# Down products one unit later, and the third low up chunk on GpSimd, in a perceiver layer with a routed expert stage

## The chip, the cores and the metric

The kernel runs on one core of one Trainium2 chip. The metric is the device time in microseconds of one execution; of several executions the median is taken. Less is better.

## What is computed

One layer over 512 tokens of width 512 (`x`), in three parts that each add to `x`:

```
x = x + cross_attention(layernorm(x), ctx 8192 x 512, bias 512 x 8192)
x = x + causal_self_attention(layernorm(x))
x = x + moe(layernorm(x))          # the part that the change touches

moe:  scores = softmax(x @ gate_w.T)            # 8 experts, the best 2 of each token
      for each expert e:  g, u = x @ gate_up[e].T       # 2 x 704 wide
                          out += w[:, e] * ((silu(g) * u) @ down[e].T)
      out += sigmoid(x @ shared_gate) * shared(x)       # a shared expert of width 1408
```

The products are float32 in accuracy. Each float32 operand is split into a high part (a rounded copy of it in the type `fp32r`) and a low part (the operand less its high part, in `fp32r` too), and a product is three matrix multiplications: high by high, high by low, low by high.

## The kernel before, in words

**Stages.** The cross attention takes the first 60% of the time, the self attention follows, and then the expert stage. The shared expert is cut in 11 slices of 128 hidden columns each; eight of them (numbers 0 to 7) come before the routed experts and three after. Between them lie the routed **units**. A unit is 128 gathered token rows of one expert: `unit(u)` exists once in the program of each engine (lines 1329 for TensorE, 1905 for VectorE, 800 for ScalarE), and for GpSimd it is one turn of a loop with `down_last_low` and `send_home`. There are 8 units for the 8 experts, and up to 7 more for experts with over 128 rows. In the profiled inputs there are 3 more, so 11 units.

**One unit.** The up and gate weights of an expert come in three chunks c = 0, 1, 2 (256, 256 and 192 hidden columns, gate and up side by side: 2048, 2048 and 1536 numbers in each partition), and so do the down weights (1024 numbers in each partition). For each unit:

- SyncE issues the loads `raw_u[c]` (1, 1 and 0.75 MB) and `raw_d[c]` (0.5 MB each). There is one buffer of each, so a load waits until the low part of the weights before it has been made (`up_lo_ready`, `dn_lo_ready`, `dn_last_ready`). All loads stand in one order in SyncE's queue (`load_unit`).
- ScalarE copies the raw weights to their high parts (`up_high`, `down_high`), applies silu (`silu_e`), copies the turned hidden values to their high part (`hidden_high`), copies the gathered rows (`gathered_high`), and copies the finished result out of PSUM (`keep`, into the one buffer `y_out`).
- VectorE makes the low parts: of the up weights (`up_low`, or in two halves `up_low_half`), of the down chunks 0 and 1 (`down_low`), of the hidden values (`hidden_low`) and of the gathered rows (`gathered_low`), and it multiplies gate by up (`product_e`). The low parts of weights read two operands from SBUF. The others read one from SBUF and one from PSUM.
- GpSimd makes the low part of down chunk 2 (`down_last_low`, line 528), and sends the finished rows home with an indirect DMA (`send_home`, line 551): it waits until the rows of the unit before have landed, casts the row numbers (`home_s`), waits for `keep`, makes a one-element addition (`blank`) and issues the DMA.
- TensorE multiplies (`up`, `down`), turns the hidden values (`turn_hidden`) and the rows of the next unit (`turn_gathered`).

**Order.** The order on each engine is written out by hand, and every engine works strictly in order. TensorE in unit u: `up(u,0)`, `down(u-1,2)`, `turn_gathered(u+1)`, `up(u,1)`, `turn_hidden(u,0)`, `up(u,2)`, `turn_hidden(u,1)`, `down(u,0)`, `turn_hidden(u,2)`, `down(u,1)`. So the down products of a unit stand in the same unit, but for the third. `down_last_low(u)` holds a wait on `up_lo_ready` that lets it start only after the first up chunk of the next unit has its low part.

**Buffers of result.** `keep(u)` waits until all three down products of unit u are done and until the rows of unit u-1 have landed at home (`y_stored`), since there is one `y_out`. TensorE's first down product of the next unit waits for `keep` (`y_ready`), since there is one PSUM bank for the result.

Of the kernel before, what the change touches and what calls it, by code (L numbers as in the profile page):

```python
# [17 lines left out]
ST = S // P  # L18
# [32 lines left out]
def perceiver_layer(nc, x_in, stream1, ctx_in, wq_in, wk_in, wq_t_in, wk_t_in, bq_in, bk_in, wv_in, wqkv_in, gate_in, shared_in, up_in,  # L51
# [3 lines left out]
    with ExitStack() as scope:  # L55
# [178 lines left out]

        def turned_hidden(c):
            return ps[:, 3 + c, 0:2 * P]
# [48 lines left out]
        dn_last_ready = sem("dn_last_ready")  # L285
# [20 lines left out]
        def _(sp):  # L306
# [95 lines left out]
            def load_unit(u, expert_, expert_before, second=False, rows=True):  # L402
# [4 lines left out]
                if not second:  # L407
                    load_down(u - 1, expert_before, 2)
# [6 lines left out]
                load_down(u, expert_, 0)  # L415
                load_down(u, expert_, 1)
# [25 lines left out]
            load_down(extra + (E - 1), sp.value_load(last_expert[0:1, 0:1], min_val=0, max_val=E - 1), 2)  # L442
# [13 lines left out]
        def _(pool):  # L456
# [103 lines left out]

            down_last_low(0)
            pool.wait_ge(home_full, 16)
            pool.wait_ge(more_ready, 1)
            final = pool.value_load(more[0:1, 0:1], min_val=0, max_val=MORE) + (E - 1)
            send_home(0, first=True)
            down_last_low(1)
# [10 lines left out]
        def _(act):  # L577
# [203 lines left out]
            def silu_e(u, c):  # L781
                act.wait_ge(up_psum, u * CH + (c + 1))
                act.activation(gated_e[:, c, 0:WIDE[c]], ps[:, c % 2, 0:WIDE[c]], ACT.Silu).then_inc(silu_e_done, 1)
# [16 lines left out]
            def unit(u, first=False, second=False, last=False):  # L800
                silu_e(u, 0)
                down_high(u, 1)
                if not first:
                    keep(u - 1, first=second)
                if not last:
                    up_high(u + 1, 0)
                else:
# [4 lines left out]
                if not first:  # L812
                    act.wait_ge(y_psum_e, u * CH)
                down_high(u, 2)
                silu_e(u, 2)
                hidden_high(u, 1)
                if not last:
                    gathered_high(u + 1)
                    up_high(u + 1, 1)
                    hidden_high(u, 2)  # L820
                    up_high(u + 1, 2)
                    act.wait_ge(y_psum_e, u * CH + 1)
                    down_high(u + 1, 0)
                else:
                    hidden_high(u, 2)
# [28 lines left out]
            for n in range(LEAD):  # L854
# [9 lines left out]
                if n == LEAD - 2:  # L864
                    act.wait_ge(down_lo_ready, RAW)
                    up_high(0, 2)
            act.wait_ge(rows_out, 16 * 2 * ST)
            down_high(0, 0)
            gathered_high(0, bank=gate_bank(LEAD - 2))
            unit(0, first=True)  # L870
            unit(1, second=True)
            final = act.value_load(more[0:1, 0:1], min_val=0, max_val=MORE) + (E - 1)
            with act.Fori(2, final) as e:
                unit(e)
            unit(final, last=True)
            shared_sides_high(SH - 1)
# [11 lines left out]
        def _(pe):  # L888
# [398 lines left out]
            def up(u, c):  # L1287
                pe.wait_ge(xg_lo_ready, u + 1)
                pe.wait_ge(up_lo_ready, u * CH + (c + 1))
                out_ = ps[:, c % 2, 0:2 * WIDE[c]]  # L1290
# [38 lines left out]
            def unit(u, first=False, last=False, ahead=False):  # L1329
                if not first:  # L1330
                    pe.wait_ge(prod_e_done, u * CH)
                up(u, 0)
                if not first:
                    down(u - 1, 2)
                if first:
                    pe.wait_ge(added, 1)
                if not last:
                    turn_gathered(u + 1, ahead=ahead)
                if first:
                    pe.wait_ge(added, ST)  # L1340
                up(u, 1)
                turn_hidden(u, 0)
                up(u, 2)
                turn_hidden(u, 1)
                if not first:
                    pe.wait_ge(y_ready, u)
                down(u, 0)
                turn_hidden(u, 2)
                down(u, 1)
# [27 lines left out]
            unit(0, first=True, ahead=True)  # L1377
            for u in range(1, AHEAD_ROWS - 1):
                unit(u, ahead=True)
# [7 lines left out]
            down(final, 2)  # L1387
# [8 lines left out]
        def _(dve):  # L1396
# [452 lines left out]
            def up_low(u, c):  # L1849
                dve.wait_ge(up_hi_ready, u * CH + (c + 1))  # L1850
                dve.tensor_tensor(wu_lo[c][:, :, :], raw_u[c][:, :, :], wu_hi[c][:, :, :].bitcast(F32),
                                  ALU.subtract).then_inc(up_lo_ready, 1)
# [21 lines left out]
            def product_e(u, c):  # L1874
                dve.wait_ge(silu_e_done, u * CH + (c + 1))
                w = WIDE[c]
                h, g_, u_ = hid_e[:, c, 0:w], gated_e[:, c, 0:w], ps[:, c % 2, w:2 * w]
# [27 lines left out]
            def unit(u, first=False, last=False):  # L1905
                if first:
                    dve.wait_ge(down_done, LEAD + CREDIT)
                    for st in (2, 0, 1, 3):
                        add_shared(st)
                product_e(u, 0)  # L1910
                down_low(u, 1)
                if not last:
                    up_low_half(u + 1, 0, False)
                product_e(u, 1)
                hidden_low(u, 0)
                if not last:
                    up_low_half(u + 1, 0, True)
                product_e(u, 2)
                hidden_low(u, 1)
                if not last:  # L1920
                    gathered_low(u + 1)
                    up_low_half(u + 1, 1, False)
                    hidden_low(u, 2)
                    up_low_half(u + 1, 1, True)
                    up_low(u + 1, 2)
                    down_low(u + 1, 0)
                else:
                    hidden_low(u, 2)
# [22 lines left out]
            down_low(0, 0)  # L1951
# [96 lines left out]
```

## Time and profile before

| | |
|---|---|
| median of 3 runs | 686.71 us (685.3 to 690.03) |
| the profiled execution | 686.13 us, its span 684.4 us |
| TensorE busy | 678.1 us, 99% of the span |
| VectorE busy | 553.8 us, 81% |
| ScalarE busy | 340.3 us, 50% |
| GpSimd busy | 211.4 us, 31% |
| DMA | 134.33 MB moved, mean 196 GB/s |
| granted TensorE clock | 1.00 (2.4 GHz) over the whole span |

The routed units lie from 515.8 us to 658.9 us of the span. How to read it: busy time is the time in which an engine's instructions ran, whether they did work or were held up by something that the profile doesn't name; an "idle before" is time in which it waited, with the engine that ended the wait. L with a number is a line of the kernel. DVE is VectorE, ACT is ScalarE, POOL is GpSimd, PE is TensorE, SP is SyncE.

### The profile page before, as it was taken

Reading aid. Unit: us, or ns where it says so; the run is one execution under the profiler, and the core shown is the slowest. Engines: PE = TensorE matmul, PEld = TensorE weight load, DVE = VectorE, ACT = ScalarE, POOL = GpSimd, SP = SyncE. Lnnn points to the kernel's source line nnn. Section 1 sums busy time; section 2 is a strip of 40 time slices with the busy share of each in tenths; the row PEclk is TensorE's granted clock in tenths of the full one; section 3 lists DMA queues with packets and bytes.
Section 4 is the critical chain, followed back from the end, with each engine's and each line's share of the span. In section 5 each row is a group of like instructions: output and inputs, shape, how many; then the busy total and the mean of one; then the engine's idle time right before and its main releaser. Section 6 shows DMA issues by size and latency. Waiting matters only on the chain.

```text
span 684.4 us, 9739 instructions
## 1 busy us (share of the span) xinstructions
PE 678.1 (99%) x3156; PEld 562.4 (82%) x3156; DVE 553.8 (81%) x722; ACT 340.3 (50%) x460; POOL 211.4 (31%) x167
## 2 busy tenths in 40 slices
PE   8999999999999999999999999999999999999997
PEld 7788888888888788888888888888888888888886
DVE  6588898777979998899998662669658998998937
ACT  5522222222245565566665342652356888888830
POOL 4754445445440000000000000225762433434360
PEclk9999999999999999999999999999999999999999
DMA  8467767767742236422320330713267999999723
GB/s 288 190 202 230 227 219 234 252 221 229 256 148 93 93 118 250 186 92 92 101 83 0 155 139 0 307 47 112 106 203 271 338 363 369 382 377 394 269 91 124
DMA packets 41742, 134.33 MB, mean 196 GB/s; under 512 B 6576, under 2 KB 13104, under 8 KB 38384
## 3 DMA queue, kind: packets, MB, share of 16 engines
q1 hardware_dynamic: 39184, 127.39, 52.8%
q0 software_dynamic: 1520, 5.05, 1.9%
q10 hardware_dynamic: 1008, 1.51, 0.7%
q8 instruction: 17, 0.28, 0.2%
q14 instruction: 13, 0.11, 0.1%
HBM read 123.78 MB, written 10.15 MB: 196 GB/s over the span
## 4 chain that ended last, share of the span: by engine, by line
PE 94%; DVE 2%; DMA 2%; ACT 1%; issue 1%; DVEq 0%; ACTq 0%; SPq 0%
PE ps L1075 26%; PE ps L1017 9%; PE ps L1018 8%; PE ps L1021 8%; PE ps L1313 5%; PE ps L912 4%; PE ps L914 4%; PE ps L913 4%; PE ps L1270 4%; PE ps L1294 3%; PE ps L1292 3%; PE ps L1293 3%; PE ps L982 2%; PE ps L929 2%; DMA raw_u<-up_in 1%; PE ps L1202 1%
## 5 line engine op out<-in xcount | busy, mean ns | idle before, releaser
L492 POOL TENSOR_TENSOR c_lo<-ring,c_hi 128x512 fp32r<-128x512 f32 x64 | 87.0, 1362 | 86.0 <-ACT c_hi L639 86.0
L639 ACT ACTIVATE c_hi<-ring 128x512 fp32r<-128x512 f32 x64 | 40.5, 633 | 128.5 <-PE ps L1021 86.0
L509 POOL TENSOR_TENSOR w_lo<-raw,w_hi 128x1024 fp32r<-128x1024 f32 x11 | 27.5, 2497 | 248.2 <-ACT w_hi L762 236.0
L1017 PE MATMUL ps<-qk_hi,c_hi 128*128 128x512 f32 x256 | 99.9, 390 | 0.0
L1018 PE MATMUL ps<-qk_lo,c_hi 128*128 128x512 f32 x256 | 99.6, 389 | 0.0
L1509 DVE TENSOR_TENSOR runmax<-runmax,att 128x512 f32<-128x512 f32 x64 | 83.9, 1311 | 3.7
L1503 DVE SCALAR_TENSOR_TENSOR att<-ring,beta,ps 128x512 f32 (+1 forms) x64 | 47.8, 746 | 26.6 <-PE ps L1021 25.6
L1021 PE MATMUL ps<-qk_hi,c_lo 128*128 128x512 f32 x256 | 68.6, 389 | 0.0
L1075 PE MATMUL ps<-p_hi,d_hi 128*128 128x512 f32 x256 | 63.8, 391 | 0.0
L1075 PE MATMUL ps<-p_hi,d_lo 128*128 128x512 f32 x256 | 63.3, 389 | 0.0
L1075 PE MATMUL ps<-p_lo,d_hi 128*128 128x512 f32 x256 | 63.2, 389 | 0.0
L775 ACT ACTIVATE wu_hi<-raw_u 128x2048 fp32r<-128x2048 f32 (+1 forms) x33 | 58.6, 1777 | 6.7 <-DMA raw_u<-up_in 5.9
L1859 DVE TENSOR_TENSOR wu_lo<-raw_u,wu_hi 128x1024 fp32r<-128x1024 f32 x40 | 51.5, 1287 | 10.0 <-ACT wu_hi L775 9.6
L665 ACT ACTIVATE d_hi<-ring 128x1024 fp32r<-128x1024 f32 x32 | 33.9, 1060 | 50.1 <-PE ps L1075 49.3
L1017 PEld LDWEIGHTS ps<-qk_hi,c_hi 128*128 128x128 f32 x256 | 48.1, 188 | 10.7 <-DVE qk_lo L1477 0.7
L1021 PEld LDWEIGHTS ps<-qk_hi,c_lo 128*128 128x128 f32 x256 | 48.1, 188 | 10.0
L1075 PEld LDWEIGHTS ps<-p_hi,d_lo 128*128 128x128 f32 x256 | 48.0, 188 | 10.0
L1075 PEld LDWEIGHTS ps<-p_hi,d_hi 128*128 128x128 f32 x256 | 47.6, 188 | 10.6 <-DVE ps L1609 0.8
L1075 PEld LDWEIGHTS ps<-p_lo,d_hi 128*128 128x128 f32 x256 | 48.1, 188 | 10.0
L1018 PEld LDWEIGHTS ps<-qk_lo,c_hi 128*128 128x128 f32 x256 | 48.1, 188 | 9.8
L1292 PE MATMUL ps<-wu_hi,xg_hi 128*128 128x512 f32 (+1 forms) x132 | 51.0, 386 | 0.0
L1294 PE MATMUL ps<-wu_hi,xg_lo 128*128 128x512 f32 (+1 forms) x132 | 49.3, 373 | 0.0
(320 smaller groups left out, 1466.9 us busy)
## 6 DMA issues: line engine op xcount, KB each, us to landing
ring<-stream SPq DMA_DIRECT2D x64, 512.0 KB, 4.3
raw_u<-up_in SPq DMA_DIRECT2D x22, 1024.0 KB, 7.0
raw_d<-down_in SPq DMA_DIRECT2D x33, 512.0 KB, 7.7
ring<-ctx_in SPq DMA_DIRECT2D x32, 512.0 KB, 3.3
raw<-shared_in SPq DMA_DIRECT2D x11, 768.0 KB, 5.8
raw_u<-up_last_in SPq DMA_DIRECT2D x11, 768.0 KB, 7.8
slots<-blank SPq DMA_DIRECT2D x15, 264.0 KB, 5.1
late<-wqkv_in SPq DMA_DIRECT2D x1, 3072.0 KB, 10.6
```

Source lines behind the costliest of these rows:

```text
L492: pool.tensor_tensor(c_lo[:, s % 2, :], ring1[:, s, 0, :], c_hi[:, s % 2, :].bitcast(F32), ALU.subtract).then_inc(lo1_ready, 1)
L639: act.activation(c_hi[:, s % 2, :], ring1[:, s, 0, :], ACT.Copy).then_inc(hi1_ready, 1)
L775: act.activation(wu_hi[c][:, :, :], raw_u[c][:, :, :], ACT.Copy).then_inc(up_hi_ready, 1)
L1017: pe.matmul(ps[:, s, :], hi, qk_hi[:, k, :], start=(k == 0), stop=False)
L1018: pe.matmul(ps[:, s, :], hi, qk_lo[:, k, :], start=False, stop=False)
L1021: return pe.matmul(ps[:, s, :], c_lo[:, s % 2, k * P:(k + 1) * P], qk_hi[:, k, :], start=False, stop=(k == KC - 1))
L1075: mm = pe.matmul(ps[:, 4 + d, :], a[s % 2][:, t, d * P:(d + 1) * P], b[s % 2][:, t, :], start=(opening and t == 0), stop=False, skip_group ...
L1292: pe.matmul(out_, xg_hi[:, k, :], wu_hi[c][:, k, :], start=(k == 0), stop=False)
L1294: mm = pe.matmul(out_, xg_lo[:, k, :], wu_hi[c][:, k, :], start=False, stop=(k == KC - 1))
L1503: dve.scalar_tensor_tensor(out=att[:, g * U + s, :], in0=ring1[:, s, 1, :], scalar=beta[:, 0:1], in1=ps[:, s, :], op0=ALU.mult, op1=ALU.ad ...
L1509: dve.tensor_tensor(runmax[:, :], runmax[:, :], att[:, g * U + s, :], ALU.max).then_inc(max_done, 1)
L1859: ins = dve.tensor_tensor(wu_lo[c][:, k, :], raw_u[c][:, k, :], wu_hi[c][:, k, :].bitcast(F32), ALU.subtract)
```

## The change

TensorE's order in unit u becomes `up(u,0)`, `turn_hidden(u-1,2)`, `down(u-1,0)`, `up(u,1)`, `turn_hidden(u,0)`, `turn_gathered(u+1)`, `up(u,2)`, `down(u-1,1)`, `turn_hidden(u,1)`, `down(u-1,2)`: all three down products of a unit stand in the next unit. The third up chunk gets a PSUM bank of its own (7). The orders of ScalarE, VectorE and SyncE follow. The low part of the third up chunk is made by GpSimd (`up_last_low`) ahead of `down_last_low`, which loses its wait on the up chunk, and `send_home` comes after both. In short (lines of waits' counts left out where they only follow the new order):

```diff
+        up_bank = (0, 1, 7)
...
# SyncE
             def load_up(u, expert_, c, first=False):
                 if not first:
-                    sp.wait_ge(up_lo_ready, u * CH + (c + 1 - CH))
+                    if c < 2:
+                        sp.wait_ge(up_lo_ready, u * 2 + (c + 1 - 2))
+                    else:
+                        sp.wait_ge(up_last_ready, u)
...
                 load_up(u, expert_, 0)
                 if not second:
-                    load_down(u - 1, expert_before, 2)
+                    load_down(u - 1, expert_before, 0)
                 load_up(u, expert_, 1)
...
                 load_up(u, expert_, 2)
-                load_down(u, expert_, 0)
-                load_down(u, expert_, 1)
+                if not second:
+                    load_down(u - 1, expert_before, 1)
+                    load_down(u - 1, expert_before, 2)
...
# GpSimd
+            def up_last_low(u):
+                pool.wait_ge(up_hi_ready, u * CH + CH)
+                pool.tensor_tensor(wu_lo[2][:, :, :], raw_u[2][:, :, :], wu_hi[2][:, :, :].bitcast(F32),
+                                   ALU.subtract).then_inc(up_last_ready, 1)
+
-            def down_last_low(u, last=False):
+            def down_last_low(u):
                 pool.wait_ge(dn_hi_ready, u * CH + CH)
-                if not last:
-                    pool.wait_ge(up_lo_ready, u * CH + (CH + 1))
...
             with pool.Fori(2, final) as e:
+                up_last_low(e + 1)
+                down_last_low(e)
                 send_home(e - 1)
-                down_last_low(e)
+            down_last_low(final)
             send_home(final - 1)
-            down_last_low(final, last=True)
             low_parts(LEAD + 1, (LEAD + 1) % RAW, (LEAD + 1) % HL)
             send_home(final)
...
# ScalarE
+            def unit(u, units_before=2, first_kept=False, last=False):
+                if units_before == 2:
+                    keep(u - 2, first=first_kept)
+                if units_before:
+                    down_high(u - 1, 1)
+                    down_high(u - 1, 2)
                 silu_e(u, 0)
+                if units_before:
+                    hidden_high(u - 1, 2)
                 if not last:
                     up_high(u + 1, 0)
+                if units_before:
+                    act.wait_ge(y_psum_e, u * CH + (1 - CH))
+                down_high(u, 0)
...
                 silu_e(u, 1)
                 hidden_high(u, 0)
+                if not last:
+                    up_high(u + 1, 1)
                 silu_e(u, 2)
+                if not last:
+                    gathered_high(u + 1)
                 hidden_high(u, 1)
                 if not last:
                     up_high(u + 1, 2)
...
# TensorE
+            def unit(u, units_before=2, last=False, ahead=False):
                 up(u, 0)
+                if units_before:
+                    turn_hidden(u - 1, 2)
+                    if units_before == 2:
+                        pe.wait_ge(y_ready, u - 1)
+                    down(u - 1, 0)
+                up(u, 1)
+                turn_hidden(u, 0)
+                if not units_before:
+                    pe.wait_ge(added, ST)
                 if not last:
                     turn_gathered(u + 1, ahead=ahead)
                 up(u, 2)
+                if units_before:
+                    down(u - 1, 1)
                 turn_hidden(u, 1)
+                if units_before:
+                    down(u - 1, 2)
...
+            turn_hidden(final, 2)
+            pe.wait_ge(y_ready, final)
+            for c in range(CH):
+                down(final, c)
...
# VectorE
             def unit(u, first=False, last=False):
...
+                else:
+                    up_low_half(u, 1, True)
                 product_e(u, 0)
+                if not first:
+                    hidden_low(u - 1, 2)
+                    down_low(u - 1, 1)
                 if not last:
+                    up_low(u + 1, 0)
                 product_e(u, 1)
                 hidden_low(u, 0)
+                down_low(u, 0)
+                product_e(u, 2)
                 if not last:
+                    gathered_low(u + 1)
                 hidden_low(u, 1)
                 if not last:
                     up_low_half(u + 1, 1, False)
```

## Rows read from the trace of the kernel before

**Rows 1.** The page: its first line, busy times, and the chain that ended last.
```profile
span 684.4 us, 9739 instructions
...
PE 678.1 (99%) x3156; PEld 562.4 (82%) x3156; DVE 553.8 (81%) x722; ACT 340.3 (50%) x460; POOL 211.4 (31%) x167
...
PE 94%; DVE 2%; DMA 2%; ACT 1%; issue 1%; DVEq 0%; ACTq 0%; SPq 0%
```

**Rows 2.** Stretches of one unit: length, busy (instructions), clock, DMA share, GB/s.
```profile
540.00:552.60 12.60, 12.60 (x65) 10.62 (x63) 11.78 (x17) 10.77 (x14) 5.32 (x5) 1.00 0.94 362
...
604.20:616.90 12.70, 12.70 (x65) 10.77 (x64) 11.76 (x17) 10.50 (x14) 5.36 (x5) 1.00 1.00 390
```

**Rows 3.** Timeline of TensorE: start us, duration us, instruction, count, idle before.
```profile
539.88 0.40 PE L1292 MATMUL ps<-wu_hi,xg_hi 128*128 128x512 f32 x1
...
542.62 0.39 PE L1313 MATMUL ps<-wd_hi,hh_e 128*128 128x512 f32 x1
...
544.11 0.48 PE L1292 MATMUL ps<-wu_hi,xg_hi 128*128 128x512 f32 x1
...
546.95 0.38 PE L1300 MATMUL ps<-ident,hid_e 128*128 128x128 f32 x2
...
552.60 0.39 PE L1292 MATMUL ps<-wu_hi,xg_hi 128*128 128x512 f32 x1
...
642.98 0.39 PE L1292 MATMUL ps<-wu_hi,xg_hi 128*128 128x512 f32 x1
```

**Rows 4.** Timeline of VectorE, from one unit's first up half to the next.
```profile
539.73 1.51 DVE L1859 TENSOR_TENSOR wu_lo<-raw_u,wu_hi 128x1024 fp32r<-128x1024 f32 x1 [0.80 <-ACT wu_hi L775]
541.16 0.28 DVE L1889 TENSOR_TENSOR hl_e<-ps,hh_e 128x128 fp32r<-128x128 f32 x1
...
541.78 1.23 DVE L1859 TENSOR_TENSOR wu_lo<-raw_u,wu_hi 128x1024 fp32r<-128x1024 f32 x1
542.92 1.75 DVE L1851 TENSOR_TENSOR wu_lo<-raw_u,wu_hi 128x1536 fp32r<-128x1536 f32 x1
544.59 1.22 DVE L1865 TENSOR_TENSOR wd_lo<-raw_d,wd_hi 128x1024 fp32r<-128x1024 f32 x1
...
552.40 1.51 DVE L1859 TENSOR_TENSOR wu_lo<-raw_u,wu_hi 128x1024 fp32r<-128x1024 f32 x1 [0.75 <-ACT wu_hi L775]
```

**Rows 5.** Timeline of GpSimd over the same time.
```profile
540.46 0.82 POOL L554 CAST home_s<-home_all 128x1 int32 x1 [0.30 <-DMA home<-y_out,home_s]
...
546.01 1.02 POOL L558 DMA_INDIRECT home<-y_out,home_s  x1 [0.15 <-issue]
...
553.70 0.25 POOL L554 CAST home_s<-home_all 128x1 int32 x1 [0.88 <-DMA home<-y_out,home_s]
```

**Rows 6.** Timelines of GpSimd and VectorE where the two overlap, in two units.
```profile
525.02 2.41 POOL L532 TENSOR_TENSOR wd_lo<-raw_d,wd_hi 128x1024 fp32r<-128x1024 f32 x1 [14.63 <-DVE wu_lo L1859]
...
525.51 0.68 DVE L1870 TENSOR_TENSOR xg_lo<-ps,xg_hi 128x512 fp32r<-128x512 f32 x1
...
601.91 2.41 POOL L532 TENSOR_TENSOR wd_lo<-raw_d,wd_hi 128x1024 fp32r<-128x1024 f32 x1 [3.70 <-DVE wu_lo L1859]
...
603.65 1.75 DVE L1859 TENSOR_TENSOR wu_lo<-raw_u,wu_hi 128x1024 fp32r<-128x1024 f32 x1 [0.50 <-ACT wu_hi L775]
```

**Rows 7.** GpSimd's line 492: duration ns min/median/max, first and last start.
```profile
L492 POOL TENSOR_TENSOR c_lo<-ring,c_hi x64: 1290/1293/1845, 24.7 to 201.3; 128x512 fp32r<-128x512 f32 x64
```

**Rows 8.** Timeline of ScalarE: a down copy, then the copy of the result.
```profile
543.10 1.05 ACT L779 ACTIVATE wd_hi<-raw_d 128x1024 fp32r<-128x1024 f32 x1
544.05 0.59 ACT L793 ACTIVATE y_out<-ps 128x512 f32<-128x512 f32 x1
```

**Rows 9.** Line 558, the indirect DMA that sends the rows home: count, and landing times.
```profile
L558 POOL DMA_INDIRECT home<-y_out,home_s x11: 1016/1016/1017, 533.3 to 660.2; - x11
...
DMA to landing us min/median/max: 2.8/7.4/7.9
```

**Rows 10.** Timeline of VectorE in the tail, behind the additions of the rows from home.
```profile
675.51 0.69 DVE L1777 TENSOR_TENSOR hid<-gated,ps 128x512 f32<-128x512 f32 x1 [0.48 <-PE ps L914]
```

More of the change, by code:

```diff
@@ L798, in gathered_high @@
                                ACT.Copy).then_inc(xg_hi_ready, 1)
-            def unit(u, first=False, second=False, last=False):
+            def unit(u, units_before=2, first_kept=False, last=False):
[4 more added lines that the diff above has]
+                    down_high(u - 1, 2)
                 silu_e(u, 0)
-                down_high(u, 1)
-                if not first:
-                    keep(u - 1, first=second)
+                if units_before:
+                    hidden_high(u - 1, 2)
                 if not last:
                     up_high(u + 1, 0)
-                else:
+                if units_before:
+                    act.wait_ge(y_psum_e, u * CH + (1 - CH))
+                down_high(u, 0)
+                if last:
                     shared_sides_high(LEAD + 1)
@@ L866, in _ @@
                     up_high(0, 2)
+            gathered_high(0, bank=gate_bank(LEAD - 2))
             act.wait_ge(rows_out, 16 * 2 * ST)
[L868 to L871, printed above, removed]
+            unit(0, units_before=0)
+            unit(1, units_before=1)
+            unit(2, first_kept=True)
             final = act.value_load(more[0:1, 0:1], min_val=0, max_val=MORE) + (E - 1)
-            with act.Fori(2, final) as e:
+            with act.Fori(3, final) as e:
                 unit(e)
             unit(final, last=True)
+            keep(final - 1)
+            down_high(final, 1)
+            down_high(final, 2)
+            hidden_high(final, 2)
             shared_sides_high(SH - 1)
@@ L1288, in up @@
                 pe.wait_ge(xg_lo_ready, u + 1)
[L1289 to L1290 removed]
+                if c < 2:
+                    pe.wait_ge(up_lo_ready, u * 2 + (c + 1))
+                else:
+                    pe.wait_ge(up_last_ready, u + 1)
+                out_ = ps[:, up_bank[c], 0:2 * WIDE[c]]
                 for k in range(KC):
@@ L1375, in _ @@
                 down_shared(n)
-            unit(0, first=True, ahead=True)
-            for u in range(1, AHEAD_ROWS - 1):
-                unit(u, ahead=True)
+            for u in range(AHEAD_ROWS - 1):
+                unit(u, units_before=min(u, 2), ahead=True)
             pe.wait_ge(more_ready, 1)
@@ L1386, in _ @@
             side_shared(LEAD, 0, gate_bank(LEAD), g_psum)
-            down(final, 2)
+            turn_hidden(final, 2)
+            pe.wait_ge(y_ready, final)
+            for c in range(CH):
+                down(final, c)
             side_shared(LEAD, 1, 2 + gate_bank(LEAD), u_psum)
@@ L1909, in unit @@
                         add_shared(st)
+                else:
+                    up_low_half(u, 1, True)
                 product_e(u, 0)
-                down_low(u, 1)
+                if not first:
+                    hidden_low(u - 1, 2)
+                    down_low(u - 1, 1)
                 if not last:
-                    up_low_half(u + 1, 0, False)
+                    up_low(u + 1, 0)
                 product_e(u, 1)
                 hidden_low(u, 0)
+                down_low(u, 0)
+                product_e(u, 2)
                 if not last:
-                    up_low_half(u + 1, 0, True)
-                product_e(u, 2)
+                    gathered_low(u + 1)
                 hidden_low(u, 1)
                 if not last:
-                    gathered_low(u + 1)
                     up_low_half(u + 1, 1, False)
[L1923 to L1928, printed above, removed]
             for n in range(LEAD):
@@ L1956, in _ @@
             unit(final, last=True)
+            down_low(final, 1)
+            hidden_low(final, 2)
             hidden(LEAD)
```

42 lines of the change are left out of this document (9 added, 33 removed).

## The prediction

> **What bounds the kernel now.** The page comes first: TensorE is busy for 99% of the span and holds 94% of the chain that ended last [rows 1]. Then the table of stretches: in the routed units TensorE is busy all the time at a granted clock of 1.00 (2.4 GHz), VectorE for 11.8 of 12.6 us, and the DMA share is 0.94 to 1.00 at up to 390 GB/s [rows 2]. So three resources are nearly full, and none has much to give. TensorE's timeline says what there is to gain: an undisturbed unit lasts 12.72 us (539.88 to 552.60), eight of them up to 642.98 last 103.1, or 12.89 each [rows 3]. Waits cost only some 0.2 us a unit.
>
> VectorE's timeline shows how full it is: from one unit's first up half to the next are 12.67 us, of which 0.75 are idle, and 0.28 are a stretched instruction (1.51 in place of 1.23) [rows 4]. Its own work is thus 12.67 - 0.75 - 0.28 = 11.64 us a unit.
>
> The last view is the overlap of VectorE and GpSimd, and it carries the forecast. At 603.65 a low part of weights took 1.75 us where 1.23 is usual, and GpSimd's subtraction, begun at 601.91, ended at 604.32: of 0.67 us of overlap 0.52 were lost. Beside the same GpSimd instruction at 525.02 VectorE's `xg_lo`, which has only one operand in SBUF, took its 0.68 us [rows 6]. The other way round, a cast of 128x1 on GpSimd took 0.25 us when VectorE was idle and 0.82 when it began 0.73 us into a low part: it ended at 541.28, and the low part at 541.24 [rows 4, 5]. I read this as exclusion: a VectorE instruction with two operands in SBUF and a GpSimd instruction don't run together; the second waits for the end of the first. So GpSimd's time is not free for VectorE's kind of work.
>
> **The change, part by part.**
>
> *Third up chunk taken from VectorE.* It frees 1.67 us (542.92 to 544.59) [rows 4]: 11.64 - 1.67 = 9.97 us of own work a unit.
>
> *The same chunk on GpSimd.* 512 numbers cost 1.29 us [rows 7], 1024 cost 2.41 [rows 6], 1.12 for each further 512: 1536 cost 3.5 us. The Trainium skill's "GPSIMD Engine Reference" (section "Elementwise — side-by-side cycle accounting") gives about 2.6 cycles an element, an estimate of 3.3 us at the 1.2 GHz that it states; the unit below would be 0.2 us shorter by it.
>
> *The lost cover.* Before, GpSimd's down low part was held back by a wait on the first up chunk, so that it lay beside VectorE's PSUM work and its idle 0.75 us. That wait goes, and the idle time goes too. GpSimd now follows ScalarE: the third up part after `up_high(u+1,2)`, which is ScalarE's last instruction of a unit, so at the start of the next unit, when VectorE has its two up halves; then the down part (2.4), then the cast and the one-element addition (0.2 each), all behind one another. What VectorE can do beside them: under the up part almost nothing, since `up_low_half(u,1)` stands at the head of its queue and everything waits behind it, `product_e(u,0)` too; under the down part `product_e(u,0)` (about 0.4, estimate from `hl_e`-sized rows) and `hidden_low(u-1,2)` (0.62, 541.16 to 541.78 [rows 4]), before `down_low(u-1,1)` is held. So VectorE is held 3.5 + (2.4 - 1.0) + 0.2 = 5.1 us a unit. **The unit: 9.97 + 5.1 = 15.0 us**, with VectorE never idle.
>
> Bounds of this: if all that VectorE reads from PSUM lay under GpSimd, only the instructions that exclude each other would count: VectorE's six halves of 1.14 (541.78 to 542.92) are 6.8, GpSimd's 3.5 + 2.4 + 0.4 are 6.3, together 13.1 us. If none did: 9.97 + 6.3 = 16.3. I take the value from the order in the diff.
>
> *TensorE's new order.* It moves work and hardly changes it. Two groups of transposes become one, and a group of products behind transposes takes 2.84 us (544.11 to 546.95) in place of 2.74 (539.88 to 542.62) [rows 3]: 0.1 us a unit, so 12.6. It gives the hidden values more time, against waits that cost 0.2. Against 15.0 this is worth nothing.
>
> *`keep` and the way home.* This is a second loop, new in the change. `keep(u-2)` stands first in ScalarE's unit and waits until the rows before have landed; behind it are two down copies; GpSimd's down part waits for the second; `send_home` comes behind that, and its landing frees the next `keep`. Once round: landing 7.4 [rows 9], `keep` 0.59, copies 0.95 and 1.05 [rows 8], down part 2.4, cast, addition and gap 0.6 = 13.0 us, above TensorE's 12.6 already. Before, the landing was hidden, though by only 0.88 us of GpSimd's wait at 553.70 [rows 5]. Into this loop VectorE's `down_low` (1.14) and the now unsplit `up_low(u+1,0)` (2.28) slip between GpSimd's instructions, which makes up to 16.4. But 7.4 was measured with a full DMA [rows 2]; the last landing, without loads beside it, took 2.8 [rows 9]. Units of 15 us need 13/15 of the traffic rate, so I take about 6, at which this loop too gives 15.0.
>
> *Loads.* The same bytes. SyncE's queue waits for the new low parts, and the order of its waits is that of the work; units of 15 us leave each buffer over 2 us more than now. Nothing added, and covered by the longer unit.
>
> *First unit, last unit, tail.* The first unit gives two down products (about 2.9 us) to the tail, which takes them back; but unit 1 can't start that much sooner, since its gathered rows are copied behind the third silu: 0 to 2.9 us lost, I take 1.8, as most of that chain stays. The last unit still has both GpSimd parts but fewer low parts on VectorE: 0 to 3.5, I take 1.8. In the tail GpSimd makes the last down part, sends a unit home, makes a shared low part, and only then sends the last unit home; the product at 675.51, behind the additions of the rows from home, has 0.48 us of slack [rows 10]: 0 to 3 us, I take 1.5.
>
> **Sum.** Nine whole units (1 to 9): 9 x (15.0 - 12.89) = 19.0; with 1.8 + 1.8 + 1.5 = 24.1 us. The profiled execution was 686.13 us, so 710.2; the median of the runs stood 0.6 above it: 711.
>
> **The rivals.** *The way home sets the unit* (the landing stays at 7.4): 16.4 us a unit, 9 x 3.5 + 5.1 = 36.7, so 723. For it: the landing is between 7.4 and 7.9 in half of the units. Against: a slower kernel empties the DMA.
>
> *Well packed*: the two engines fit into each other at 13.1 to 14.3 a unit, so 2 + 2 to 13 + 4, or 691 to 704. For it: VectorE may do its two halves first, since they come before `up_high(u+1,2)` is ready. Against: the third up part then still meets a queue of two-operand work.
>
> *No exclusion, and so not slower*: the lost 0.52 us is a share of something slower, half speed for each. The overlap of 0.67 would then have cost 0.34, not 0.52, and GpSimd's 5.9 us would cost VectorE under 3: 9.97 + 2.6 = 12.6, TensorE's own. It decides from a VectorE unit under 12.6 us on. Then each unit saves 0.29 at best, 9 x 0.29 = 2.6, and it is 684. Against: rows 5 and 6 end together to 0.04 us. The Trainium skill, "SBUF — State Buffer", section "Who interferes with whom", states the same: whichever starts first gets the shared pair for the whole instruction, and the other fully blocks. The trace agrees by the 0.52 us of rows 6; by a half-speed share it would be 684, by the rule 711.
>
> That the change doesn't do what it says I can exclude: the subtraction stands plainly in GpSimd's queue.
>
> **How the numbers follow.** Forecast 0.50 (704 to 717); way home 0.20 (717 to 726); well packed 0.16 (691 to 704, under 694 in 0.03); no exclusion 0.08 (682 to 688); something above 726, as a load that comes late behind the new waits, 0.06. The range 694 to 726 leaves out 0.03 + 0.08 below and 0.06 above. 1% (6.9 us) is about what a measurement of this kernel can tell from no change: faster needs 680, which only an unseen gain would give, 0.02; same (to 693.6) is the rest of "no exclusion" and the foot of "well packed", 0.10; slower 0.88.
>
> **What would show it.** In the timeline of VectorE each unit has a first or second half of `wu_lo` of chunk 1 with some 3 to 4.6 us in place of 1.2, a `wd_lo` of over 2 us, and no idle time; GpSimd's new row of 128x1536 lasts 3.5 us, its small ones 1 us or more; TensorE waits in each unit for `wu_lo` ahead of `up(u,1)`, 2.4 us a unit in all; the DMA share falls to about 0.85 and the landing of line 558 to about 6 us. If `keep` (line 793) waits for the landing in each unit, the second loop rules. I am wrong if VectorE's two-operand rows keep 1.2 us beside GpSimd's, or if the units keep 12.6 us.

## The result, and the profile after

The changed kernel takes 720.27 us (median of 6 runs, 718.23 to 721.55), against 688.25 for the kernel before in the same comparison: a ratio of 1.047, with an interval of 1.044 to 1.050. It is slower by some 32 us, against 24 forecast. The profiled execution took 719.24 us, 33.1 above that of before.

The first lines of the page, after, with the chain that ended last (their counterparts are [rows 1]):

```profile
span 717.1 us, 9744 instructions
...
PE 686.3 (96%) x3156; PEld 565.3 (79%) x3156; DVE 575.8 (80%) x702; ACT 338.0 (47%) x460; POOL 263.3 (37%) x177
...
PE 71%; issue 11%; POOL 10%; DVE 3%; DMA 3%; ACT 1%; POOLq 0%; DVEq 0%; ACTq 0%; SPq 0%
```

TensorE has lost its hold on the chain, 71% in place of 94%, and GpSimd, which was not in it, has 10%. The stretches of four units, after (columns as in [rows 2]: length, then the busy time of TensorE, of its weight loads, of VectorE, ScalarE and GpSimd, the granted clock, the DMA share and GB/s):

```profile
572.60:589.10 16.50, 14.57 (x64) 12.01 (x65) 14.55 (x16) 10.03 (x14) 10.08 (x5) 0.90 0.85 295
589.10:604.60 15.50, 13.02 (x65) 10.59 (x63) 13.89 (x14) 11.43 (x15) 10.14 (x6) 1.00 0.82 304
604.60:620.70 16.10, 13.14 (x64) 10.74 (x64) 14.12 (x15) 10.60 (x14) 10.05 (x5) 1.00 0.87 314
...
636.00:653.30 17.30, 14.52 (x63) 12.04 (x64) 14.57 (x16) 10.06 (x15) 11.12 (x5) 0.90 0.89 333
```

These four units last 15.5 to 17.3 us; all nine from unit 1 on last 14.4 to 17.3, 15.7 in the mean. TensorE is no longer full, the DMA share, 0.94 to 1.00 before, is 0.82 to 0.89, and VectorE is busy for about 14 us, yet not for all of the unit. So no engine bounds this kernel by its own busy time. The table of waits, after, from 527 to 670 us (engine, line, what was waited for, and from whom: us in total, times, longest), says what does:

```profile
ACT y_out L807 <- DMA home<-y_out,home_s: 29.5, 8, 5.1
...
PE ps L1335 <- ACT y_out L807: 13.3, 7, 2.8
DVE hid_e L1900 <- ACT gated_e L797: 11.7, 8, 2.2
...
PE ps L1314 <- DVE xg_lo L1892: 6.2, 7, 1.8
```

ScalarE's `keep` (line 807 now) waits in nearly every unit for the rows on their way home, 3.7 us each time, and TensorE's down products wait for `keep`. That is a ring, and one turn of it can be read off two timelines. ScalarE, after, from one `keep` to the next:

```profile
593.27 0.60 ACT L807 ACTIVATE y_out<-ps 128x512 f32<-128x512 f32 x1 [3.38 <-DMA home<-y_out,home_s]
593.77 2.00 ACT L793 ACTIVATE wd_hi<-raw_d 128x1024 fp32r<-128x1024 f32 x2
...
609.35 0.60 ACT L807 ACTIVATE y_out<-ps 128x512 f32<-128x512 f32 x1 [4.90 <-DMA home<-y_out,home_s]
```

GpSimd, after, over the same unit (its counterparts are [rows 5]):

```profile
589.99 3.46 POOL L538 TENSOR_TENSOR wu_lo<-raw_u,wu_hi 128x1536 fp32r<-128x1536 f32 x1 [3.44 <-ACT wu_hi L789]
595.84 2.41 POOL L543 TENSOR_TENSOR wd_lo<-raw_d,wd_hi 128x1024 fp32r<-128x1024 f32 x1 [2.40 <-ACT wd_hi L793]
598.19 1.19 POOL L565 CAST home_s<-home_all 128x1 int32 x1
599.52 2.06 POOL L568 TENSOR_TENSOR blank<-blank 128x1 f32<-128x1 f32 x1
601.74 1.01 POOL L569 DMA_INDIRECT home<-y_out,home_s  x1 [0.15 <-issue]
```

And VectorE, after, over it (counterparts in [rows 4]):

```profile
588.89 5.64 DVE L1881 TENSOR_TENSOR wu_lo<-raw_u,wu_hi 128x1024 fp32r<-128x1024 f32 x2
596.07 0.42 DVE L1900 TENSOR_TENSOR hid_e<-gated_e,ps 128x256 f32<-128x256 f32 x1 [1.54 <-ACT gated_e L797]
...
597.03 2.30 DVE L1887 TENSOR_TENSOR wd_lo<-raw_d,wd_hi 128x1024 fp32r<-128x1024 f32 x1
599.26 2.28 DVE L1873 TENSOR_TENSOR wu_lo<-raw_u,wu_hi 128x2048 fp32r<-128x2048 f32 x1
```

`keep` and two copies: 593.27 to 595.77. The down part, to 598.25. Then the two operations on one element: the cast is issued at 598.19 and ends at 599.38, with VectorE's `wd_lo`, which ends at 599.33; the addition begins at 599.52 and ends at 601.58, with VectorE's `wu_lo`, which ends at 601.54. Two instructions that need 0.2 us each have cost 3.3. The indirect DMA is issued at 601.74 and its rows have landed 7.6 us later, when `keep` starts at 609.35: a turn of 16.08 us. VectorE pays too: its two halves last 5.64 us in place of 2.35, beside GpSimd's 3.46, and its `wd_lo` 2.30 in place of 1.23, beside GpSimd's down part. Yet it also idles 1.54 us, for `silu`, which stands in ScalarE's queue behind `keep`.

The indirect DMA's landing times over all units, after (counterpart in [rows 9]):

```profile
DMA to landing us min/median/max: 2.8/6.9/8.0
```

### The profile page after: what moved, and what is told of

It reads as the page before. It is cut to its first block, busy times and chain, and to the rows that moved or that the text cites. A ratio compares the mean times of both kernels' runs of the same rounds, so it can differ in the third digit from the quotient of the medians.

```text
span 717.1 us, 9744 instructions
## 1 busy us (share of the span) xinstructions
PE 686.3 (96%) x3156; PEld 565.3 (79%) x3156; DVE 575.8 (80%) x702; ACT 338.0 (47%) x460; POOL 263.3 (37%) x177
## 4 chain that ended last, share of the span: by engine, by line
PE 71%; issue 11%; POOL 10%; DVE 3%; DMA 3%; ACT 1%; POOLq 0%; DVEq 0%; ACTq 0%; SPq 0%
PE ps L1094 24%; PE ps L1036 8%; PE ps L1037 8%; PE ps L1040 8%; POOL wu_lo L538 5%; PE ps L931 3%; PE ps L933 3%; PE ps L932 3%; PE ps L1289 3%; POOL home_s L565 2%; PE ps L1001 2%; PE ps L948 2%; POOL home L569 1%; PE ps L1221 1%; POOL wd_lo L543 1%
## 5 line engine op out<-in xcount | busy, mean ns | idle before, releaser
L1314 PE MATMUL ps<-wu_hi,xg_hi 128*128 128x512 f32 (+1 forms) x132 | 52.6, 399 | 8.8 <-DVE xg_lo L1892 6.2
L1881 DVE TENSOR_TENSOR wu_lo<-raw_u,wu_hi 128x1024 fp32r<-128x1024 f32 x20 | 56.2, 2854 | 0.0
L538 POOL TENSOR_TENSOR wu_lo<-raw_u,wu_hi 128x1536 fp32r<-128x1536 f32 x10 | 39.0, 3895 | 44.6 <-ACT wu_hi L789 44.6
```

What stands on the lines that cost most here:

```text
L538: pool.tensor_tensor(wu_lo[2][:, :, :], raw_u[2][:, :, :], wu_hi[2][:, :, :].bitcast(F32), ALU.subtract).then_inc(up_last_ready, 1)
L1314: pe.matmul(out_, xg_hi[:, k, :], wu_hi[c][:, k, :], start=(k == 0), stop=False)
L1881: ins = dve.tensor_tensor(wu_lo[c][:, k, :], raw_u[c][:, k, :], wu_hi[c][:, k, :].bitcast(F32), ALU.subtract)
```

## Where the 33 us lie

Two more rows of TensorE's timeline before, the first `up` of unit 1 and the shared slice behind the last unit:

```profile
527.22 0.39 PE L1292 MATMUL ps<-wu_hi,xg_hi 128*128 128x512 f32 x1
...
655.08 0.39 PE L912 MATMUL ps<-l_hi,w_hi 128*128 128x512 f32 x1
```

After, the rows that stand at the same places are at 526.47, at 667.80 (unit 10's first `up`, 642.98 before [rows 3]) and at 681.58.

| stretch | before | after | difference |
|---|---|---|---|
| to unit 1's start | 527.22 | 526.47 | -0.75 |
| units 1 to 9 | 115.76 | 141.33 | +25.6 (2.84 a unit) |
| unit 10 | 12.10 | 13.78 | +1.7 |
| the rest | 29.3 | 35.5 | +6.2 |

The first and the last line share the two down products (2.9 us) that have gone from the first unit to the tail: less those, the first unit lost 2.15 and the tail 3.3.

## Experiments

The names: **the read cost** is VectorE held by GpSimd's subtractions, **the way home** is the ring above. Ratios are to the kernel before, run beside each.

**1. Rows home ahead of the down part.** In GpSimd's loop of the changed kernel:

```diff
                 up_last_low(e + 1)
-                down_last_low(e)
                 send_home(e - 1)
+                down_last_low(e)
```

> The changed kernel, but GpSimd sends a unit home ahead of the down low part of the next, in place of behind it. Nothing else moves. Theory 'way home' (the unit of 15.7 us is the loop: landing, keep, two down copies, down part on GpSimd, cast and addition held behind VectorE, indirect DMA, landing): the down part and the copies leave the loop, which falls to about 10 to 12 us, and the unit falls to what VectorE needs, 15.7 less its idle 1.3: about 14.4 to 15.0 us, some 709 to 713 us in all. ScalarE's wait for the landing ahead of keep goes. Theory 'exclusion alone' (VectorE, held by GpSimd, sets the unit): the same low parts are made in the same time, so the units stay at 15.7 us and the time at 720 us.

Measured: 714.81 us, ratio 1.040 (1.038 to 1.042). `keep` no longer waits for the landing. The stretch from 560 to 650 of this run (columns as in [rows 2]):

```profile
560.00:650.00 90.00, 77.25 (x367) 61.08 (x366) 89.30 (x84) 63.85 (x82) 50.40 (x29) 1.00 0.84 316
```

Two rows of VectorE's timeline in it:

```profile
602.58 5.66 DVE L1881 TENSOR_TENSOR wu_lo<-raw_u,wu_hi 128x1024 fp32r<-128x1024 f32 x2
...
610.26 4.48 DVE L1873 TENSOR_TENSOR wu_lo<-raw_u,wu_hi 128x2048 fp32r<-128x2048 f32 x1
```

VectorE is busy 89.3 of 90 us and the units last 15.3 in the mean. The second bound lay just under the first: take the ring away and VectorE, held by GpSimd, sets nearly the same time. Unit 1 to unit 10 takes 137.5 us (527.03 to 664.54), 3.8 less than in the changed kernel. The spans of the two profiled executions differ by 6.0 us (717.1 and 711.1): these 3.8, and 2.7 behind the units, less 0.6 lost ahead of them.

**2. The up part back on VectorE**, all else as changed:

```diff
# GpSimd
-                up_last_low(e + 1)
# VectorE, unit(u)
                     hidden_low(u - 1, 2)
+                    up_low(u, 2)
                     down_low(u - 1, 1)
```

> The changed kernel, but with the third up low part back on VectorE (behind the hidden low part at the start of a unit); down products stay one unit late, and send_home stays behind the down part. Theory 'way home': the up part on GpSimd isn't in the loop, and VectorE's low parts still slip in between the down part, the cast and the addition, so the unit stays at 15 us or more: 712 to 720 us. Theory 'exclusion alone': GpSimd holds VectorE for only 1.4 us a unit, 11.64 + 1.4 + 0.2 = 13.2 us a unit: 691 to 696 us.

Measured: 731.72 us, 1.063 (1.060 to 1.067). Slower than the change, outside what either theory said. GpSimd's timeline in this run:

```profile
599.32 2.40 POOL L543 TENSOR_TENSOR wd_lo<-raw_d,wd_hi 128x1024 fp32r<-128x1024 f32 x1 [9.63 <-ACT wd_hi L790]
601.66 1.72 POOL L565 CAST home_s<-home_all 128x1 int32 x1
603.52 1.00 POOL L568 TENSOR_TENSOR blank<-blank 128x1 f32<-128x1 f32 x1
604.68 2.88 POOL L569 DMA_INDIRECT home<-y_out,home_s  x1 [0.15 <-issue]
```

VectorE's, beside the last of these rows:

```profile
604.39 2.28 DVE L1870 TENSOR_TENSOR wu_lo<-raw_u,wu_hi 128x2048 fp32r<-128x2048 f32 x1
```

`keep` to `keep` is 17.7 us here. VectorE's extra chunk has put one more long instruction where the ring passes, so that now the indirect DMA itself runs beside one: 2.88 us in place of 1.01, 2.4 in the mean of the eleven. Its landing, counted from the issue, goes to 9.6. VectorE meanwhile is idle for about 5 us a unit. With one buffer and the rows behind the down part, the ring sets the unit, and giving work back to VectorE lengthens it.

**3. The up part on GpSimd in the order of before**, `down_last_low` keeping its wait:

```diff
             with pool.Fori(2, final) as e:
                 send_home(e - 1)
                 down_last_low(e)
+                up_last_low(e + 1)
```

> The kernel before, in its own order, but with the third up low part on GpSimd, behind the down low part (which keeps its wait). So one half of the change alone. Theory 'way home': send_home follows keep at once as before and the landing stays covered, so the units grow only by what GpSimd holds VectorE: the up part falls at the start of a unit beside product, down part 1 and up half: up to 3.5 us held, 1.67 saved: 12.9 to 14 us a unit, 688 to 700 us. Theory 'exclusion alone': this half is all of the loss, 15 us or more a unit, 708 to 720 us.

Measured: 711.93 us, 1.033 (1.028 to 1.039). There is no wait for the way home here. A row of VectorE in this run:

```profile
636.88 4.50 DVE L1873 TENSOR_TENSOR wu_lo<-raw_u,wu_hi 128x1024 fp32r<-128x1024 f32 x1
```

And GpSimd's beside it:

```profile
636.80 3.49 POOL L533 TENSOR_TENSOR wu_lo<-raw_u,wu_hi 128x1536 fp32r<-128x1536 f32 x1 [1.91 <-ACT wu_hi L786]
```

TensorE then waits 1.8 to 1.9 us a unit for that half. So the move of one subtraction costs 24 us, with none of the new order. Not all of it is the wait itself. Six of the nine units last 14.6 to 14.7 us, at a granted clock of 1.00; the other three last 16.3, at a mean granted clock of 0.89 to 0.90, and TensorE is busy 1.6 us longer in each. That is about 5 of the 24 us. One of the four executions, with a mean clock of 0.997 where the profiled one had 0.990, took 705.84 us.

**4. The same with a fill in place of the up part** (that low part is left out of the result; slices shortened here):

```diff
-                pool.tensor_tensor(wu_lo[2], raw_u[2], wu_hi[2], ALU.subtract)
+                pool.tensor_tensor(blank[:, 2:3], blank[:, 2:3], blank[:, 3:4], ALU.add)
+                pool.memset(wu_lo[2], 0.0)
```

> The kernel before in its own order, with the third up low part replaced by GpSimd's memset (left out, nothing read). So VectorE gets its 1.67 us a unit back and GpSimd holds nobody. It tells what the relief of VectorE would be worth without exclusion: TensorE has only some 0.3 us a unit to give and the DMA is full, so 683 to 687 us; against offload_alone's 712 us the rest is what GpSimd's reads cost.

Measured: 684.9 us, 0.9965 (0.9948 to 0.9981); units of 12.6, TensorE busy 90.0 of 90 us. Taking 1.67 us of work a unit from VectorE is worth 2.4 us in all, since TensorE is the bound; doing that work on GpSimd, in place of the fill, costs 27, with the 5 us of clock in it. The fill is also shorter (1.39 us for 3.49), so this alone doesn't part reading from length; the row of experiment 5 does.

**5. The fill in the changed kernel.**

> The changed kernel, but GpSimd fills the third up low part with zeros (a memset of 128x1536, which reads nothing from SBUF, behind a one-element addition) in place of computing it: the low part is left out, and GpSimd is held for about 1.3 us there in place of 3.5. Exclusion by reads: VectorE's low parts that lie beside the memset take their usual 1.2 us each, not stretched. Exclusion of the whole engine: they are stretched by the memset's time. The unit: the way home still sets it, 14.5 to 16 us, so 708 to 720 us; if VectorE alone set it, some 12.5 to 13 us and 686 to 695 us.

Measured: 712.26 us (one run). VectorE's two halves in this run:

```profile
600.15 2.35 DVE L1881 TENSOR_TENSOR wu_lo<-raw_u,wu_hi 128x1024 fp32r<-128x1024 f32 x2
```

And the fill on GpSimd beside them:

```profile
600.10 1.37 POOL L539 MEMSET wu_lo<- 128x1536 f32 x1
```

The fill started first and lies wholly beside them, and adds nothing: a write holds nobody, reads do. And the kernel is still 25 us slower than before, with VectorE idle for up to 5.9 us ahead of one `product_e` a unit. In the units `keep` starts 15.0 to 16.9 us apart, each time behind the landing. So in the changed kernel the read cost of the up part was mostly hidden under the ring: two bounds of the same height, and neither shows its worth while the other stands.

**6. The wait taken from `down_last_low` in the kernel before.**

```diff
-                if not last:
-                    pool.wait_ge(up_lo_ready, u * CH + (CH + 1))
```

> The kernel before, with only the wait on the first up chunk taken from down_last_low. The down part then runs as soon as its high part is there, beside VectorE's two-operand low parts in place of beside its PSUM work. Exclusion: VectorE is held by up to 2.4 us a unit more, less its idle 0.75 us: 12.9 to 14 us a unit, 688 to 700 us. Without exclusion: no difference, 687 us.

Measured: 696.71 us, 1.013 (1.010 to 1.017). Units alternate between 12.6 and 14.75. In the long kind GpSimd's instruction starts first, in the short kind VectorE's. VectorE's row in one of each:

```profile
580.55 3.43 DVE L1857 TENSOR_TENSOR wu_lo<-raw_u,wu_hi 128x1024 fp32r<-128x1024 f32 x1
...
594.65 1.22 DVE L1857 TENSOR_TENSOR wu_lo<-raw_u,wu_hi 128x1024 fp32r<-128x1024 f32 x1
```

GpSimd's in the same two:

```profile
580.50 2.39 POOL L530 TENSOR_TENSOR wd_lo<-raw_d,wd_hi 128x1024 fp32r<-128x1024 f32 x1 [2.04 <-ACT wd_hi L777]
...
595.22 2.92 POOL L530 TENSOR_TENSOR wd_lo<-raw_d,wd_hi 128x1024 fp32r<-128x1024 f32 x1 [1.73 <-ACT wd_hi L777]
```

At 580.50 GpSimd starts, VectorE 0.05 us later, and VectorE takes 1.22 + 2.2. At 594.65 VectorE is first, by 0.57 us, and GpSimd takes 2.92 for 2.39. This is the exclusion at its cleanest. The wait that the change deleted was worth 9.5 us.

**7. Both bounds taken out**: rows home first, the up part back on VectorE; the late down products stay.

> The changed kernel with both suspects taken out: GpSimd sends a unit home ahead of the down low part, and the third up low part is back on VectorE. What stays of the change is the order with the down products one unit late. Theory 'two loops' (the way home at 15.9 us a unit, and below it VectorE held by GpSimd's reads at 15.4): both are gone, and the unit is VectorE's own 11.64 us and what the uncovered down part holds it for, 1.4 to 1.9: 13.0 to 13.6 us, 690 to 697 us. If the late down products themselves cost the time (theory 'order'), the units stay over 14.5 us and the time over 708 us.

Measured: 700.05 us, 1.018 (1.015 to 1.021), units of 12.8 to 14.4, 13.9 in the mean: slower than expected, so something more was in it. VectorE is busy 82.8 of 90 us, the DMA share is 0.92. ScalarE waits 19.3 us in 14 waits for loads of up weights between 555 and 650. What holds this kernel over 13 us a unit was not separated.

**8. Rows home first, and the fill.**

> The changed kernel with the unit sent home ahead of the down part, and with GpSimd's third up low part replaced by a memset that reads nothing (the low part is left out, GpSimd is busy for 1.4 us there). Against home_first (15.4 us a unit) only GpSimd's reads are gone. Theory 'two loops': the unit falls to 12.6 to 13.3 us, where TensorE, the DMA and VectorE's 9.97 + 2.4 meet: 684 to 694 us. If the loads' order holds home_first at 15.4 us (ScalarE waits for raw_u there), the unit stays above 14.5 us and the time above 705 us.

Measured: 698.25 us, 1.016 (1.013 to 1.019), units of 13.45 once the first few are past. Against experiment 1 the up part's reading is worth 16.6 us in this order. The rest was open: 0.85 us a unit over 12.6. TensorE waited 0.6 of it for `xg_lo`.

**9. The gathered rows ahead of an up copy** in experiment 8. The thought: `xg_lo` is late because ScalarE copies the rows behind `up_high(u+1,1)`, which waits for a load.

```diff
-                if not last:
-                    up_high(u + 1, 1)
                 silu_e(u, 2)
                 if not last:
                     gathered_high(u + 1)
+                    up_high(u + 1, 1)
```

> home_first_write_only (13.45 us a unit; third up low part left out, memset in its place), with one thing moved on ScalarE: the high part of the next second up chunk stands behind the third silu and the copy of the gathered rows, in place of ahead of them. Theory 'rows behind a load' (ScalarE waits 1.3 us for raw_u there, so the gathered rows are late, and TensorE waits 0.6 us for xg_lo at each unit's start): this wait of TensorE goes and the unit falls to 12.6 to 13.0 us, 686 to 691 us. Theory 'full DMA' (the DMA at a share of 0.98 sets 13.4 us): the wait only moves to another load, the unit stays, 697 us.

Measured: 694.92 us, 1.0115 (1.009 to 1.014), 3 us less, but the later units keep their 13.45, and TensorE its wait for `xg_lo`. What shows in the units is in unit 1: 12.9 us at a granted clock of 1.00, where experiment 8 had 14.3 at 0.88. The theory fell. VectorE's timeline in this run shows what stands ahead of `xg_lo`:

```profile
598.66 3.60 DVE L1886 TENSOR_TENSOR wd_lo<-raw_d,wd_hi 128x1024 fp32r<-128x1024 f32 x1
602.18 2.28 DVE L1872 TENSOR_TENSOR wu_lo<-raw_u,wu_hi 128x2048 fp32r<-128x2048 f32 x1
```

GpSimd's beside it:

```profile
597.70 1.02 POOL L569 DMA_INDIRECT home<-y_out,home_s  x1 [0.46 <-issue]
598.76 2.41 POOL L543 TENSOR_TENSOR wd_lo<-raw_d,wd_hi 128x1024 fp32r<-128x1024 f32 x1
```

**10. The same reorder in experiment 7.**

> home_first_up_dve (14.0 us a unit, the right result), with the same move on ScalarE. Theory 'rows behind a load': the unit falls by the 1.0 us for which TensorE waits for xg_lo, until VectorE's own 11.64 us and the uncovered down part (1.5 to 2.4) hold it: 13.1 to 13.6 us a unit, 691 to 696 us. Theory 'full DMA': it stays at 700 us. The kernel before (687 us) isn't beaten in either.

Measured: 701.25 us, 1.020 (1.018 to 1.022): no gain.

**11. No GpSimd reads at all**: experiment 8 with a second fill, for the down part (both low parts are left out; slices shortened here).

```diff
-                pool.tensor_tensor(wd_lo[2], raw_d[2], wd_hi[2], ALU.subtract)
+                pool.tensor_tensor(blank[:, 4:5], blank[:, 3:4], blank[:, 3:4], ALU.add)
+                pool.memset(wd_lo[2], 0.0)
```

> The changed kernel's late order with the rows sent home first, and on GpSimd two fills that read nothing in place of both low parts of weights (third up chunk and third down chunk are left out of the result). Theory 1, the 13.45 us units of the same kernel with one fill come from VectorE's wd_lo being held 3.6 to 3.75 us by GpSimd's down part: wd_lo falls back to 1.2 us, the units to 12.6, and nine units save 7.7: 690 to 692 us. Theory 2, the late order itself (ScalarE's rows, the loads behind the late down parts) sets 13.45: the units stay within 0.2 us of it and the time at 697 to 699.

Measured: 690.13 us, 1.0036 (1.0019 to 1.0053). VectorE's `wd_lo` at the same place of the unit:

```profile
595.97 1.23 DVE L1887 TENSOR_TENSOR wd_lo<-raw_d,wd_hi 128x1024 fp32r<-128x1024 f32 x1
```

It is back from 3.60 to 1.23, and units 2 to 5 last 12.6 us each. So the 13.45 came from the down part on GpSimd, and the full DMA doesn't set it: its share is 0.90 to 1.01 in these four. The late order by itself costs little in the units, though not nothing. Unit 1 lasts 14.3, at a granted clock of 0.88, units 8 and 9 last 13.5 and 13.7, where TensorE waits 0.8 us for `xg_lo` and ScalarE 2.0 to 2.1 us for a load of up weights, and all nine take 117.4 us, 1.65 more than before.

**The account.** Each step adds one thing to the one before:

| kernel | us | step |
|---|---|---|
| before | 687 | |
| late down products, rows home first, no reads by GpSimd (11) | 690.1 | 3: the order |
| with the down part, uncovered (8) | 698.3 | 8: its reading |
| with the up part (1) | 714.8 | 17: its reading |
| rows home behind both: the change | 720.3 | 5.5: the way home |

The steps depend on their order, as experiment 5 shows: with the ring in place the up part's reading is worth 8 us (720.3 less 712.3), not 17. The two "reading" steps each put a subtraction in place of a shorter fill; that it is the reading that holds VectorE is shown by the fill's row in experiment 5. No version that computes all of the result beats the kernel before.

## Why the prediction was right, and where it was off

**The exclusion** was right, in mechanism and in size. One case with 0.67 us of overlap had carried it [rows 6]; the halves of 5.64, the 4.50 of experiment 3 and the pair of experiment 6 repeat it with whole instructions, in both directions. Which of the two engines is held doesn't always follow from their recorded starts (last section). One row of the reading was misread: the cast of 0.25 us at 553.70 didn't meet an idle VectorE, since the low part begun at 552.40 ran until 553.91 [rows 4, 5]. It ended 0.04 us behind that, so it bears the exclusion out too; alone, such a cast takes 0.18 us (688.04, after). The Trainium skill ("SBUF — State Buffer", section "Who interferes with whom") says that such a VectorE instruction contends with a GpSimd instruction that reads SBUF, not with one that only writes it. By that rule the fill beside the halves costs nothing, and the trace agrees: 2.35 us with it and without.

**VectorE's unit of 15.0 us** was nearly right as a bound, and wrong as the thing that sets the time. Experiment 1, where it does set it, has 15.3: the up part lasted 3.51 to 4.56 us there, 3.8 in the mean, where I had 3.5, since it too is held when a VectorE half starts first. In the changed kernel VectorE was busy for 14.2 us a unit, the time held included, and idle for 0.1 to 2.7 us, 1.5 in the mean; "VectorE never idle" was false.

**The way home** is the step that failed. I had built the ring with the right links and made its two ends 13.0 and 16.4 us, and then took 15.0 with a landing of "about 6", worked out from a DMA with less traffic. The traffic fell as said (share 0.82 to 0.89 in the four units shown, forecast 0.85), and the landing hardly moved: 6.9 in the median of all eleven from 7.4. In the ring it didn't fall at all: from the issue to `keep`'s start the seven turns between 553.92 and 656.47 have 6.8 to 8.0 us, 7.4 in the mean; the median is drawn down by the last ones, from 664.94 on. The other term was near its upper end: VectorE's two instructions slipped in between GpSimd's small ones as allowed for, 3.3 us for the cast and the addition. So the rival of chance 0.20 set the unit, at 15.70 in place of its 16.4, and the time lies in that rival's 717 to 726 and outside the 704 to 717 of the forecast itself. That it is off by only 9 us is in part luck: the two bounds happened to have nearly the same height (15.3 and 15.7 us a unit). Nine units came to 25.6 us in place of 19.0, and that is most of the 9 us between forecast and measurement. The sign to look for was written down, `keep` waiting for the landing in each unit, and it is there.

**TensorE's waits** were forecast ahead of `up(u,1)`, for a low part. There was one such wait in units 1 to 9, of 1.4 us. They are instead for `keep` (13.3 us in 7) and for `xg_lo`. In three of the nine units the mean granted clock was 0.89 to 0.90: for a few us it stood at the lower level of 1.2 GHz (0.53 from 577.70 to 580.40), behind gaps in TensorE's work of 1.77, 1.93 and 2.75 us. Gaps of 1.70, 2.04 and 2.36 us, ahead of 593.92, 561.98 and 610.18, left it at 1.00, so the length of one gap doesn't tell which. TensorE's busy time was 14.5 to 14.6 us in these units, 13.0 to 13.2 in the others. The ring wasn't longer for it: `keep` to `keep` took 16.2 and 15.3 us over the second and third of them, 15.4 to 16.5 over the other turns behind 561. In experiment 1 the clock was 1.00 throughout.

**The small terms.** First unit 2.15 (forecast 1.8), last unit 1.7 (1.8), tail 3.3 (1.5). Of the tail, 0.64 us are TensorE's wait for the last down part, and VectorE waits 2.36 us for the last rows from home. "Loads: nothing added" held: ScalarE waited for a load of up weights 5.6 us in all between 527 and 670.

**"TensorE's new order hardly changes anything"** nearly held: experiment 11 has units of 12.6 us in it, and costs 3 us in all.

**The rivals.** Well packed: no, since the up part lies under VectorE's halves and not between them. No exclusion: no, by any of the runs. Its sum was also off: half of GpSimd's 5.9 us is 2.95, not 2.6, so VectorE's unit would have been 12.9, as long as the unit before, and the time 687 rather than 684.

## What to carry over

GpSimd is no spare engine for VectorE's subtractions: a GpSimd subtraction that reads SBUF takes up to its whole time from VectorE's two-operand instructions (3.3 of 3.5 us in experiment 3), unless a wait puts it beside VectorE's PSUM work, and such a wait is worth keeping even if it looks idle. When a result leaves through one buffer, add up the ring (copy out, whatever the sending engine does first, issue, landing, back to the copy) before anything is put ahead of the send, and price each tiny instruction in it at the length of the longest instruction that can block it. Take a landing from the rows at a loaded DMA; it doesn't shrink in proportion to traffic.

## What the runs showed of the hardware

An indirect DMA's issue on GpSimd is held by VectorE's two-operand subtraction, where that runs already: 2.88 us in place of 1.01 beside one in experiment 2, ending 0.89 us behind it, and 2.4 in the mean of the eleven issues. Where the issue starts first it isn't: in the kernel before, the issue at 546.01 took 1.02 us, and VectorE's `wd_lo`, begun at 546.18, its usual 1.22. A longer issue stands in the kernel before too, where four such issues follow one another and the third runs beside a `wu_lo`:

```profile
494.92 0.96 POOL L525 DMA_INDIRECT slots<-rows_n,row_of  x1 [0.31 <-issue]
496.19 2.49 POOL L525 DMA_INDIRECT slots<-rows_n,row_of  x1 [0.30 <-issue]
```

VectorE's, beside the second of these rows:

```profile
495.57 2.28 DVE L1851 TENSOR_TENSOR wu_lo<-raw_u,wu_hi 128x2048 fp32r<-128x2048 f32 x1
```

The Trainium skill, on the page named above, infers that such a subtraction doesn't stall a DMA (it takes only the read side of the shared pair, and writing descriptors needs the write side). These rows don't decide on that: an indirect DMA also takes its row numbers from SBUF (`home_s`, `row_of`), and no run here parts the reading of them from the writing of descriptors. What they do show is that an indirect DMA in a send path can be held.

The recorded starts don't always tell which of the two engines is held. In experiment 6 VectorE starts 0.57 us ahead of a GpSimd that was idle, and GpSimd is held. In experiment 9 VectorE's `wd_lo` at 598.66 starts 0.10 us ahead of GpSimd's down part, during the issue of the indirect DMA, and yet it is VectorE that takes 3.60 us. In experiment 1 there are seven such pairs, with VectorE up to 0.54 us ahead (551.42 against 551.96), and VectorE takes 3.85 to 4.01 us for its 1.23, while GpSimd's subtraction keeps its 2.4. In all of them the issue stands directly ahead of GpSimd's subtraction. Why VectorE loses its lead there is open; it makes the down part cost VectorE 2.3 to 2.8 us in experiments 1, 8 and 9, all of GpSimd's instruction or more.
